# Joint powers of two norms on GpSimd, and up products between down products, in a block of FFN, recurrence and FFN

## The reference

```python
def ternary_linear(x, w):                  # EPS = 1e-8
    alpha = mean(abs(w)); w_t = sign(w) * (abs(w) > 0.5 * alpha)
    rms = sqrt(sum(x * x, -1)) / sqrt(d)
    return einsum('bsd,fd->bsf', x / (rms + EPS), w_t)
def ffn(x): return ternary_linear(gelu(ternary_linear(x, w_up)), w_down)
def rnn(x):                                # in log space in the original
    f, i = sigmoid(x @ Wf.T), sigmoid(x @ Wi.T); h = g(x @ Wh.T)   # g(x) = x + 0.5 or sigmoid(x)
    return scan(s = f * s + i * h, s0 = 0.5)                       # over time
x = x + 0.5 * ffn(layernorm(x))            # x: 32 x 256 x 128, d_ff = 512
x = x + rnn(layernorm(x))
x = x + 0.5 * ffn(layernorm(x))
```

## Time and profile before

| | |
|---|---|
| median of 3 runs | 262.69 us (262.29 to 263.86) |
| the profiled execution | 263.04 us, span 261.3 us |
| PE busy (matmul) | 236.6 us, 91% |
| DVE busy | 234.1 us, 90% |
| ACT busy | 221.4 us, 85% |
| POOL busy | 216.4 us, 83% |

### The profile page before, as it was taken

One profiled execution on the slowest core, in us unless ns is written; L12 is line 12 of the kernel. 1 busy time (PEld: TensorE's weight loads), 2 busy tenths in 40 slices (PEclk: granted clock), 3 DMA queues, 4 the chain that ended last, 5 costly groups with the idle time before them and its releaser, 6 DMA issues.

```text
span 261.3 us, 9753 instructions
## 1 busy us (share of the span) xinstructions
PE 236.6 (91%) x3759; PEld 167.1 (64%) x3759; DVE 234.1 (90%) x754; ACT 221.4 (85%) x534; POOL 216.4 (83%) x400
## 2 busy tenths in 40 slices
PE   0759999999998899899999998679999999999992
PEld 0626777777777667655555544357777776777782
DVE  3798799999999998999999999986999999988784
ACT  2377999989998899879999997997899999999861
POOL 5676998989998898599999999998889989997133
PEclk9988999999999999999999999999999999999999
DMA  6990000000000000000000000000111211112114
GB/s 188 300 265 3 4 4 3 3 3 4 3 3 4 3 4 4 3 0 1 3 1 0 0 1 3 3 3 3 43 43 57 67 46 43 43 43 82 46 43 123
DMA packets 18062, 9.73 MB, mean 37 GB/s; under 512 B 608, under 2 KB 17888, under 8 KB 18016
## 3 DMA queue, kind: packets, MB, share of 16 engines
q1 hardware_dynamic: 17744, 8.98, 12.5%
q10 hardware_dynamic: 272, 0.13, 0.2%
HBM read 4.92 MB, written 4.19 MB: 35 GB/s over the span
## 4 chain that ended last, share of the span: by engine, by line
PE 53%; DVE 21%; ACT 7%; POOL 7%; issue 6%; DVEq 0%; ACTq 0%; POOLq 0%
PE Y L502 17%; PE U L458 9%; PE G L489 9%; PE U L459 8%; DVE hidden L701 5%; PE T L439 4%; ACT h_hi L330 4%; DVE st L719 3%; DVE h_lo L654 3%; PE U L518 2%; DVE cand L691 2%; DVE mv L619 2%; PE G L478 2%; POOL xn L236 2%; POOL root L212 2%
## 5 line engine op out<-in xcount | busy, mean ns | idle before, releaser
L654 DVE SCALAR_TENSOR_TENSOR h_lo<-h_hi,U 128x1024 f16<-128x1024 f16 x63 | 75.6, 1215 | 10.0 <-ACT h_hi L330 9.6
L324 ACT ACTIVATE U<-U 128x1024 f32<-128x1024 f32 x63 | 64.7, 1026 | 15.3 <-PE U L459 14.4
L236 POOL TENSOR_SCALAR xn<-X,neg_mean,rstd 128x128 f32<-128x128 f32 x156 | 67.8, 447 | 6.9 <-DVE rstd L624 4.2
L330 ACT ACTIVATE h_hi<-U 128x1024 f16<-128x1024 f32 x63 | 64.7, 1027 | 1.0
L502 PE MATMUL Y<-down_w,h_hi 128*128 128x128 f16 x496 | 59.4, 220 | 0.0
L502 PE MATMUL Y<-down_w_half,h_lo 128*128 128x128 f16 x496 | 59.0, 219 | 0.0
L458 PE MATMUL U<-xt_hi,up_w 128*128 128x512 f16 x128 | 49.2, 384 | 9.4 <-DVE h_lo L654 7.5
L212 POOL TENSOR_TENSOR root<-mv,half 128x8 f32<-128x8 f32 x31 | 51.0, 1644 | 2.3
L459 PE MATMUL U<-xt_lo,up_w 128*128 128x512 f16 x128 | 49.2, 384 | 0.0
L502 PEld LDWEIGHTS Y<-down_w_half,h_lo 128*128 128x128 f16 x496 | 48.5, 98 | 0.4
L502 PEld LDWEIGHTS Y<-down_w,h_hi 128*128 128x128 f16 x496 | 47.7, 98 | 1.6
(11 more groups left out here) (101 smaller groups left out, 415.2 us busy)
## 6 DMA issues: line engine op xcount, KB each, us to landing
X<-in_L_attn_x SPq DMA_DIRECT2D x16, 256.0 KB, 5.3
out_x<-X SPq DMA_DIRECT2D x15, 256.0 KB, 2.8
up_raw<-in_L_ffn_w_up SPq DMA_DIRECT2D x1, 256.0 KB, 4.5
down_raw<-in_L_ffn_w_down SPq DMA_DIRECT2D x1, 256.0 KB, 4.7
out_x<-X SPq DMA_DIRECT2D x1, 128.0 KB, 1.9
out_x<-X ACTq DMA_DIRECT2D x1, 128.0 KB, 2.9
gate_raw<-in_L_attn_Wh SPq DMA_DIRECT2D x1, 64.0 KB, 3.7
gate_raw<-in_L_attn_Wi SPq DMA_DIRECT2D x1, 64.0 KB, 3.6
```

Source lines behind the costliest of these rows:

```text
L236: m = eng.tensor_scalar(xn[:, n % 2, t, :], X[:, c, :], neg_mean[l][:, c:c + 1], rstd[l][:, c:c + 1], ALU.add, ALU.mult)
L324: eng.activation(U[part][:], U[part][:], ACT.Gelu, scale=1.0 / XN_SPLIT).then_inc(gelu_done, 1)
L330: eng.mul(h_hi[:, F % 2, 2 * part:2 * part + 2, :], U[part][:], H_SPLIT).then_inc(h_hi_done, 1)
L654: vec.scalar_tensor_tensor(out=h_lo[:, F % 2, 2 * part:2 * part + 2, :], in0=h_hi[:, F % 2, 2 * part:2 * part + 2, :], scalar=-1.0 / H_SPL ...
```

## The change

1. Joint power. For eleven groups in each FFN pass the root for the down scaling of group F is taken in the same POOL instruction as the LN deviations of the group five later (`rides_with`, `rider`): `ln_roots` works on three columns instead of two, its sum gives two denominators, and `scales` takes both reciprocals. `rms_step` and `scale_y` remain for the other ten groups (`alone`). On DVE, `scales(0, k+3)` stands between the two `h_low` of step k, and `stats(0, k+4)` at the end of step k.
2. Head: another order of the first steps on DVE and POOL.
3. Turn into the recurrent stage: the gates of the first two groups stand before the last gram and down products of the first pass, with other PSUM banks (`z`); group 14's diagonal is picked by DVE; the following DVE and ACT steps are written out.
4. `up_within_down` holds for groups 4 to 15 and 20 to 31.
5. End: the last gram is made chunk by chunk between the down products of group 30; group 30's rows are added by POOL and DVE in halves and stored in two pieces.

The core of the diff:

```diff
+        def rides_with(F):
+            l, k = (0, F) if F < groups else (2, F - groups)
+            return (l, k + 5) if k + 5 < groups else None
+
+        def rider(l, g):
+            return None if g < 5 else g - 5 if l == 0 else g - 5 + groups
+
+        alone = [F for F in range(2 * groups) if not rides_with(F)]
...
+        def y_factor(F, t):
+            if not rides_with(F):
+                return y_scale[:, F % 4, t:t + 1]
+            l, g = rides_with(F)
+            return scale[l][:, g * TILES + t, 1:2]
+
+        def y_ready(engine, F):
+            if rides_with(F):
+                l, g = rides_with(F)
+                engine.wait_ge(rstd_done[l], g + 1)
+            else:
+                engine.wait_ge(y_scale_done, alone.index(F) + 1)
+
...
         def diagonal_by_max(F):
-            return F >= 2 * groups - 4
+            return F >= 2 * groups - 4 or F == groups - 2
 
         def up_within_down(F):
-            return 2 * groups - 4 <= F < LAST
+            return 3 <= F < groups - 1 or groups + 3 <= F < LAST
 
...
             def ln_roots(l, g):
-                if l == 0 or g >= BY_ACT:
-                    ln_moments(l, g)
+                F = rider(l, g)
+                w = 2 if F is None else 3
                 pool.wait_ge(var_set[l], 2 * (g if l == 0 else g + 1))
-                eng.tensor_tensor(root[l][:, g % 2], mv[l][:, cols(g), 1:3], half[:], ALU.pow).then_inc(root_done[l], 1)
+                if F is not None:
+                    pool.wait_ge(ssq_done, F + 1)
+                eng.tensor_tensor(root[l][:, g % 2, :, 0:w], mv[l][:, cols(g), 1:1 + w], half[:, :, 0:w],
+                                  ALU.pow).then_inc(root_done[l], 1)
                 pool.wait_ge(root_done[l], g + 1)
-                eng.tensor_tensor(den[l][:, g % 2], root[l][:, g % 2, :, 0], root[l][:, g % 2, :, 1],
-                                  ALU.add).then_inc(den_done[l], 1)
+                if F is None:
+                    eng.tensor_tensor(den[l][:, g % 2, :, 0], root[l][:, g % 2, :, 0], root[l][:, g % 2, :, 1],
+                                      ALU.add).then_inc(den_done[l], 1)
+                else:
+                    pool.wait_ge(floor_set, 2)
+                    eng.tensor_tensor(den[l][:, g % 2], root[l][:, g % 2, :, 0::2], root[l][:, g % 2, :, 1::2],
+                                      ALU.add).then_inc(den_done[l], 1)
 
...
@@ -254,32 +296,51 @@
                 eng.tensor_tensor(inject[:, g % 2, :], sig_i[:, g % 2, :], cand[:, g % 2, :], ALU.mult).then_inc(inject_done, 1)
 
             gram_constants()
+            for l in (0, 2):
+                eng.memset(root[l][:, :, :, 3], 2.0 * H_SPLIT * RMS_EPS).then_inc(floor_set, 1)
             first_roots()
+            ln_moments(0, 1)
             ln_roots(0, 1)
             norm(1)
+            ln_moments(0, 2)
             ln_roots(0, 2)
-            for s in range(0, 3 * groups):
+            for g in range(2, 4):
+                norm(g)
+                ln_moments(0, g + 1)
+                ln_roots(0, g + 1)
+            ln_moments(0, 5)
+            for s in range(2, 3 * groups):
                 k, r, q = s, s - groups, s - 2 * groups
-                if 0 <= k - 2 < groups - 1:
+                if 2 <= k < groups - 3:
+                    ln_roots(0, k + 3)
+                elif groups - 3 <= k < groups:
                     rms_step(k - 2)
-                if 0 <= q - 2 < groups:
-                    rms_step(q - 2 + groups)
-                if s + 2 < 3 * groups:
+                if 1 <= q < groups - 3:
+                    ln_roots(2, q + 3)
+                elif groups - 3 <= q:
+                    rms_step(groups + q - 2)
+                if s + 2 < 3 * groups and r != 1:
                     norm(s + 2)
+                if r == 0:
+                    rms_step(groups - 2)
                 if 0 <= r < groups:
                     inject_step(r)
-                if s == groups:
+                if r == 0:
+                    norm(s + 3)
+                if r == 1:
                     rms_step(groups - 1)
                 if 0 <= s - 12 < groups:
                     rnn_scales(s - 12)
-                if k + 3 < groups:
-                    ln_roots(0, k + 3)
-                if 0 <= s - 28 < groups:
+                if k + 4 < groups:
+                    ln_moments(0, k + 4)
+                if 0 <= s - 28 < BY_ACT:
                     ln_roots(2, s - 28)
+                if 0 <= q < groups - 4:
+                    ln_moments(2, q + 4)
             rms_step(2 * groups - 2)
             rms_step(2 * groups - 1)
             pool.wait_ge(scaled_done, 1)
-            eng.tensor_tensor(X[:, cols(groups - 2), :], X[:, cols(groups - 2), :], scaled, ALU.add).then_inc(pool_added, 1)
+            eng.tensor_tensor(X[:, tiles - 8:tiles - 6, :], X[:, tiles - 8:tiles - 6, :], scaled[:, 0:2, :], ALU.add).then_inc(pool_added, 1)
 
...
+            def mask(F):
                 for n in range(2):
-                    pe.matmul(D[n * HALF:(n + 1) * HALF, :, 0:HALF], ident16[:, n * HALF:(n + 1) * HALF], off_diag[:],
+                    pe.matmul(gram_of(F)[n * HALF:(n + 1) * HALF, :, 0:HALF], ident16[:, n * HALF:(n + 1) * HALF], off_diag[:],
                               start=True, stop=False, tile_position=(0, n * HALF))
...
+            def products(F, t, c, last):
+                for right in (h_hi, h_lo):
+                    for n in range(2):
+                        e = slice(t * P + n * HALF, t * P + (n + 1) * HALF)
+                        m = pe.matmul(gram_of(F)[n * HALF:(n + 1) * HALF, t, 0:HALF], h_hi[:, F % 2, c, e], right[:, F % 2, c, e],
+                                      start=False, stop=last and right is h_lo, tile_position=(0, n * HALF))
+                return m
+
+            def last_gram(c):
+                pe.wait_ge(h_lo_done, 2 * LAST + max(c, 1))
+                if c == 0:
+                    mask(LAST)
+                for t in range(TILES):
+                    m = products(LAST, t, c, t == TILES - 1 and c == chunks - 1)
+                if c == chunks - 1:
+                    m.then_inc(gram_done, 1)
 
...
+            def gate(g, n):
+                if n == 0:
+                    pe.wait_ge(xt_taken, groups + g + 1)
+                if g == 0:
+                    pe.wait_ge(h_lo_done, 2 * groups - 1 if n < 2 else 2 * groups)
+                elif g == 1:
+                    if n == 0:
...
-                    if g == 1 and n >= 1:
-                        pe.wait_ge(ffn_added, groups - 2 + n)
-                    pe.matmul(Z[g % 2][n], gate_w[:, n, :], xt[:, g % 2, :], start=True, stop=True).then_inc(gate_ready, 1)
+                pe.matmul(z(g)[n], gate_w[:, n, :], xt[:, g % 2, :], start=True, stop=True).then_inc(gate_ready, 1)
...
@@ -549,19 +660,32 @@
             pe.wait_ge(limit_done, 2)
             up(0, 1)
             for k in range(1, groups):
-                up(k, 0)
+                if not up_within_down(k - 1):
+                    up(k, 0)
                 turn(k + 1)
                 up(k, 1)
                 gram(k - 1)
-                down(k - 1)
-            for r in range(groups):
+                if up_within_down(k):
+                    down(k - 1, range(0, 2))
+                    up(k + 1, 0)
+                    down(k - 1, range(2, TILES))
+                else:
+                    down(k - 1)
+            turn(groups + 1)
+            for n in range(3):
+                gate(0, n)
+            gate(1, 0)
+            turn(groups + 2)
+            gate(1, 1)
+            gate(1, 2)
+            gram(groups - 1)
+            down(groups - 1)
+            turn_back(0)
+            for r in range(2, groups):
                 turn(groups + r + 1)
-                gates(r)
-                if r >= 1:
-                    turn_back(r - 1)
-                if r == 0:
-                    gram(groups - 1)
-                    down(groups - 1)
+                for n in range(3):
+                    gate(r, n)
+                turn_back(r - 1)
             up(groups, 0)
             turn(2 * groups + 1)
             up(groups, 1)
@@ -577,10 +701,16 @@
                     down(groups + k - 1, range(0, 2))
                     up(groups + k + 1, 0)
                     down(groups + k - 1, range(2, TILES))
-                else:
+                elif k < groups - 1:
                     down(groups + k - 1)
-            gram(2 * groups - 1)
-            down(2 * groups - 1)
+            down(LAST - 1, [0])
+            last_gram(0)
+            last_gram(1)
+            last_gram(2)
+            down(LAST - 1, [1])
+            last_gram(3)
+            down(LAST - 1, [2, 3])
+            down(LAST)
 
         @block.vector
...
             def scales(l, g):
                 dve.wait_ge(den_done[l], g if l == 0 else g + 1)
-                vec.reciprocal(rstd[l][:, cols(g)], den[l][:, g % 2]).then_inc(rstd_done[l], 1)
+                if rider(l, g) is None:
 ```

(142 more changed lines are left out.)

175 lines of the change are left out of this document (107 added, 68 removed).

## The result

The changed kernel took **272.81 us** (median of four runs, 272.45 to 272.83) where the kernel before took 262.62 beside it: a ratio of 1.0377, with a 95% interval of 1.0347 to 1.0406. The forecast was 273.0. The profiled execution took 272.83 with a span of 271.0, so 9.7 us of span are to be found.

| stretch | before us | after us | difference | forecast |
|---|---|---|---|---|
| start to second `h_low` of group 3 | 35.27 | 36.41 | +1.14 | +1.61 |
| group 3 to group 12 | 51.57 | 60.81 | +9.24 | +9.18 |
| group 12 to group 15 | 17.17 | 17.26 | +0.09 | 0 |
| group 15 to `cand` of recurrent group 3 | 16.61 | 15.66 | -0.95 | 0 |
| `cand` 3 to `cand` 15 | 43.60 | 44.81 | +1.21 | 0 |

A forecast was written before the change was run, and what follows sets the result against it. POOL was taken to pace the first pass and the middle of the second, DVE the recurrent stage. 263.04 + 10.8 - 0.2 - 0.3 = 273.3 us; with the profiled execution 0.35 above the median, 273.0, range 266.5 to 277.

The forecast's parts named there:

- The power: POOL, joint instruction: twelve elements in a partition take 2.28 us, on a line through four at 1.01 and eight at 1.644.
- rival 3: POOL's joint power costs 1.65 us (total 266.6) or 2.66 us (total 276.7); chance 0.08 for something near either end.
- The chain of the first pass: First pass, reciprocal to next reciprocal through DVE and POOL: closes once a group, 6.75 us each; the pass loses 10.8 us.
- Rivals 1 and 2: First pass: POOL chain hides, 261 us, chance 0.08; both passes: PE paces at 5.31 a group, 258 us, chance 0.08.
- the first link: Start of the first pass: `mean_var(0, 6)` at 33.21 as before, so the second `h_low` of group 3 at 36.89.
- Rival 4, the clock: First pass: TensorE's clock falls while PE waits 1.5 us in each group, up to 35 us more; chance 0.03.
- eight at 5.6 and three at 5.31 make 60.7: Second pass, eleven group periods: 60.7 us against 60.86 before, so 0.2 us gained.
- The loop: Second pass, two groups through turn, ACT, DVE and up products: 11.2 us, 5.6 a group, until DVE has no statistics left.
- I take 0: Turn into the recurrent stage: no change, with 1 us either way, as DVE is already full and its work stays.
- Rival 5, a new wait there: In the turn, between the gates and the last gram: 1 to 4 us more, 275 to 277; chance 0.08.
- The end: End of the kernel: last gram about 0.7 us earlier, but only 0.3 us gained, between 0 and 0.7.

## Why the prediction was right

**The power** lay on the line: 2.277 us for twelve elements, forecast 2.28, so rival 3 falls. The Trainium skill, GPSIMD Engine Reference, section 3.1, has about 2.6 cycles an element for an elementwise operation on two inputs; this trace disagrees for the power, with 2277 - 1646 = 631 ns for four more elements in a partition.

**The chain of the first pass** was right in its links and its sum: 60.81 us for nine periods, forecast 60.75. That it is the cause is shown by the run that opens it (51.47 us, with POOL's and PE's orders untouched) and by the one that takes a link of 0.28 out of it and gains 0.28 a group. Rivals 1 and 2 fall with the ten waits at the reciprocal and grams 6.76 apart. The forecast put the second `h_low` of group 12 at 97.64; it came at 97.22. The difference is in the first link: `mean_var(0, 6)` started at 32.67 in the profiled execution and not at 33.21. That is no error of order: in the runs with the old end and with the second pass as before, which leave the head as it is, it started at 33.28 and 33.02 and the second `h_low` of group 3 at 37.03 and 36.76, around the forecast 36.89. In these two the granted clock was 0.66 between 17 and 22 us, as in the profiled execution of the kernel before; in that of the changed kernel it was 1.00 (last section). So the head was forecast right for like clocks. The Trainium skill, Perfetto Trace Analysis, section Optimization Strategies, advises to optimise the engines that block the critical path when the matmul engine idles. PE does idle here, for 1.22 us before a turn; but the run with the statistics moved made no engine's work faster, and it gave back 9.3 us between groups 3 and 12.

**Rival 4, the clock.** It fell where it was placed: the granted clock stays 1.00, the upper level (2.4 GHz), through a stretch in which PE is busy for 49.60 of 60.80 us.

**The second pass.** The step that failed is "eight at 5.6 and three at 5.31 make 60.7", -0.2 for +0.64. The loop was right in the steady groups: grams 5.31 and 5.90 apart in turn, 5.6 in the mean, and 5.31 from group 26 on. What the term left out is one period of 6.44 between the grams of groups 18 and 19, where the up products first come amid the down products. They are now asked for before the `h_low` of the group before them is done, and PE stands idle for 0.98:

```profile
197.80 0.38 PE L538 MATMUL U<-xt_hi,up_w 128*128 128x512 f16 x1 [0.98 <-DVE h_lo L787]
```

The run without the edit has 5.55 there, so this period too comes with PE's order; that run sets the price of the whole part at 1.5 us. Without the edit the rest of the change runs the stretch in 59.99 against 60.86, so 0.87 gained by the rest (POOL's lighter group, I take it, which was not tried alone) and 1.51 lost by PE's order make the 0.64.

**The turn.** The term "I take 0" was +0.26 up to `cand` 15: 0.95 gained before recurrent group 3 and 1.21 given back after it. The first four periods of `cand` from 3 on, the steps with five tiles of statistics, take 3.72, 3.73, 3.72 and 4.12 us where the kernel before took 3.53 with four: statistics put off, not work saved. But the turn's last link was mis-sized: at the start of the second pass 0.84 is gained, because `add_rnn(15)` moved ahead of a round of statistics and the gram no longer waits for it. The prediction has no term for that edit, and so left out that PE writes the tile that the addition reads. The run that moves it back shows it, and shows that the gain goes through to the end, since the rest of that pass is as long (61.50). Rival 5, a new wait there, fell.

**The end.** -0.83 for -0.3, above the bounds of 0 to 0.7. The step held in its mechanism: the last gram comes 0.67 earlier, forecast 0.7, and part of it is lost again behind it. Counted from the gram of group 30, DVE's last instruction ends at 7.54 us where it ended at 7.66; by the run without it the gram in pieces gives 0.45, and the rest of the new end, the third addition among it, costs 0.33. What the term left out is the stores: behind that instruction they take 2.62 us where the kernel before took 3.35 in its one profiled execution. Other executions with the same end take up to 3.00, so the rest of the gain is theirs; whether it is the smaller last pieces or the spread of the stores was not tried.

**The sum** came out right partly because errors cancel, which is luck: -0.5 at the head, +0.2 in the first pass, +0.3 in the turn, -0.8 at the start of the second pass, +0.8 in it and -0.5 at the end make -0.5 on a forecast of 273.3, against 272.83. The first of them is the clock's. None of them touches the sign or the main term.

## What to carry to other kernels

When a step is moved earlier in an engine's program, draw the loop that it closes: from its result through the other engines back to the next one's input, and count over how many iterations it runs. If that sum is above what the busiest engine wants for an iteration, all engines show idle time and the loop sets the pace; one more round of distance between producer and consumer added no work and gave back 9.3 us here. And ask of every edit to one engine's order which buffer it frees for another.
